# A decoder layer in five overlapped stages: row maxima turned by VectorE and DRAM, setup moved, and matmuls that nobody reads

## The chip, the cores and the metric

The kernel runs on one core of a Trainium2 chip. The metric is the device time of one execution in microseconds (us), lower is better. Engines are called as in the profile: PE (TensorE's matmuls), PEld (its weight loads), DVE (VectorE), ACT (ScalarE), POOL (GpSimd), SP (SyncE, which issues all DMAs here).

## What is computed

x is (32, 256, 256), ctx_1024 is (32, 120, 256). Cut to what matters:

```python
def attn(x):                       # 16 heads of 16, scores of rank 32, causal
    q, k, v = (split_heads(x @ W.T + b) for W, b in ((Wq, bq), (Wk, bk), (Wv, bv)))
    q_lr = einsum('bhtd,hdr->bhtr', q, Wq_lsr); k_lr = einsum('bhtd,hdr->bhtr', k, Wk_lsr)
    a = softmax(where(causal, -inf, einsum('bhir,bhjr->bhij', q_lr, k_lr) / sqrt(32)))
    return merge_heads(einsum('bhij,bhjd->bhid', a, v)) @ Wo.T + bo
def xattn(x, ctx):                 # as given: softmax over the support, then a mask on its rows
    ...
    return out @ proj_w.T + proj_b
def ffn(x):                        # x_prev is x shifted by one token
    r = sigmoid((mu_r * x + (1 - mu_r) * x_prev) @ W_r)
    k = (mu_k * x + (1 - mu_k) * x_prev) @ W_k
    return r * (square(relu(k)) @ W_v)
x = layernorm(x + attn(x)); x = layernorm(x + xattn(x, ctx)); x = layernorm(x + ffn(x))
```

## The kernel before

The 32 batches (256 tokens each) pass through five stages that are skewed against each other. In step t the kernel does IN (projections q and k) for batch t, SCORES for batch t-2, PROBS for t-3, CROSS (output projection, layer norm, cross attention) for t-4 and FFN for t-5. So steps 0 to 4 fill the pipeline, 5 to 31 are full, 32 to 36 (and a rest on the other engines) drain it. Every engine has its own program, the order of which is written out by hand, and the engines meet at semaphores; `Batch.dma_count` and `chunks_done` give the counts. `run_steps` calls `step(t)` and, after step 0, `between`, in which the remaining weights are prepared.

Scores. q and k of a batch (`rows_out_split`, line 474) are split into a high and a low part (ACT `split_hi`, line 675; DVE `split_lo`, line 873), stored to DRAM (`save_parts`, 328) and loaded back as rows per head (`load_stack`, 336, 12 DMAs of 128 KB) into `stack`. PE computes scores in six chunks (`slot`, 522, called in the order 0, 2, 3, 1, 4, 5). In a slot the stage SCORES fills `ps_s` for one batch, from which DVE takes row maxima (`row_maxima`, line 869), and PROBS fills `ps_t` for the batch before it, with the scores turned, from which ACT takes exp (line 673). Each of the two has one buffer of two banks, so a chunk waits for the reader of the one before. The negated maximum of each query, the shift, is part of the PROBS matmul: two rows (its high and its low part) at `ONES_ROW` of `stack[0]` for each half of the heads.

The way of the shift. `row_max` is [128, tile, half, head pair]. After slot 5, PE turns it with two transposes into a bank of `ps_m` (line 623), DVE negates it and splits it (lines 974 to 982) in `shift_parts`, 16 partitions by 2 by 256, and SP issues four DMAs of 8 KB from there into the two rows of each half (line 374). PE's ps_t chunk 0 of the next step waits for them (line 532). Behind them in SP's order stand the 12 loads of `stack` for the batch in stage IN.

Between the slots PE does the projections and the work of CROSS and FFN into two banks `ps_m`, whose users follow each other in a fixed ring (`BANK_USERS`, `bank_free`, line 250). After slot 5 come r3, g, the transposes mT, `PV(0)`, v3, z2, `PV(1)`, kx and vx. `xT` low parts are made by POOL (`x_lo`, line 1065) from ACT's high parts (`x_hi`).

Setup. PE folds the rank matrices and Wq (lines 402 to 417), behind a wait for the bias columns; POOL makes the identity, the block diagonal, constants, the rows of ones of slot 0 of the ring, and the masks, and then x_lo(0). After step 0, `other_weights`: PE folds Wxk with Wxq (427) and makes two constant rows (437 to 441), DVE splits Wv, Wo, Wr, Wkf, Wvf (806, 809) and copies banks (818). SP's step starts with the store of q and loads x of the next batch after the store of k (359).

Of the kernel before, what the change touches and what calls it, by code (L numbers as in the profile page):

```python
# [5 lines left out]
F32 = mybir.dt.float32  # L6
F32R = mybir.dt.float32r
# [18 lines left out]
VW = 32  # L26

# [18 lines left out]
def decoder_layer(nc, x, x_turned, ctx_turned, mask_in, Wq, bq, WkT, bk, WvT, bv, WoT, bo, Wq_lsr_turned, Wk_lsr_turned,  # L46
# [8 lines left out]
    with es:  # L55
# [42 lines left out]
        row_max = sb("row_max", [P, NT, 2, HEADS // 2])  # L98
        shift_parts = sb("shift_parts", [HEADS, 2, T], F32R)
        shift = shift_parts[:, 1, :].bitcast(F32)  # L100
# [13 lines left out]
        BLOCK = 32  # L114
# [46 lines left out]

        ps_s = ps("ps_s", [P, 1024])
# [11 lines left out]
        filled = sems(*["f_" + n for n in ("q", "k", "v", "mT", "z1", "x1T", "s2", "g", "z2",  # L174
# [16 lines left out]
        v_ = sems("q_lo", "k_lo", "shift_done", "shift_hi", "shift_lo",  # L191
# [13 lines left out]
        stack_loaded = [sem(f"stack_loaded{r}") for r in range(RING)]  # L205
        shift_loaded = [sem(f"shift_loaded{r}") for r in range(RING)]
# [23 lines left out]
        def wait(eng, s, count):  # L230

            if count > 0:
# [7 lines left out]
             ("mT", SCORES, v_["shift_done"]), ("z2", CROSS, v_["sum2_done"]), ("vx", PROBS, a_["vx_ready"])],  # L240
# [49 lines left out]
        def run_steps(step, ahead=0, between=None):  # L290

            for t in range(B + LAST_SKEW + ahead):
                step(t)
                if t == 0 and between:
                    between()
# [3 lines left out]
        def _(sp):  # L299
# [46 lines left out]
            def step(at):  # L346
                b = Batch(at, IN)
                if live(at, IN):
                    save_parts(b, 0, "q_lo")
# [7 lines left out]
                if live(at + 1, IN):  # L357
                    sp.wait_ge(g_["xT_lo"], b.n + 1)
                    sp.dma_start(x_in[:], tokens(x_turned, b.n + 1).rearrange("(k p) t -> p k t", p=P)).then_inc(x_loaded, 16)
# [4 lines left out]
                if live(at, SCORES):  # L364
# [25 lines left out]
        def _(pe):  # L390
# [16 lines left out]
            pe.wait_ge(bias_loaded, 16 * 2)  # L407
# [7 lines left out]
            bank = setup_bank()  # L415
            for a in range(KC):
# [5 lines left out]
            def other_weights():  # L422
# [11 lines left out]
                pe.wait_ge(w_ready, len(SPLIT))  # L434
# [7 lines left out]
                assert bank_no[0] == SETUP_TOTAL  # L442
                pe.wait_ge(setup_taken, SETUP_TOTAL)

# [72 lines left out]

            def step(at):
                A, Sb, Pb, X, F = (Batch(at, s) for s in (IN, SCORES, PROBS, CROSS, FFN))
                on = {s: live(at, s) for s in (IN, SCORES, PROBS, CROSS, FFN)}  # L520

                def slot(c):

                    if on[SCORES]:
# [5 lines left out]
                    if on[PROBS]:  # L530
                        if c == T_ORDER[0]:
                            pe.wait_ge(shift_loaded[Pb.slot], Pb.dma_count(4))
# [3 lines left out]
                    if on[SCORES]:  # L536
                        causal_mask(c, ps_s, mask_s, P).then_inc(s_filled, 1)
                    if on[PROBS]:
# [27 lines left out]
                slot(0)  # L566
                if on[IN]:
                    bank = bank_free(pe, "q", at)
                    pe.wait_ge(g_["xT_lo"], A.n + 1)
                    rows_out_split(bank, "Wq", xT[A.slot]).then_inc(filled["f_q"], 1)  # L570
                slot(2)
                if on[CROSS]:
# [3 lines left out]
                slot(3)  # L576
                if on[FFN]:
# [3 lines left out]
                if on[IN]:  # L581
                    bank = bank_free(pe, "k", at)
                    rows_out_split(bank, "Wk", xT[A.slot]).then_inc(filled["f_k"], 1)
# [575 lines left out]
```

## Time and profile before

| | us |
|---|---|
| median of 3 runs | 996.53 (995.14 to 1000.03) |
| the profiled execution | 1001.48 |
| its span, first to last instruction | 999.80 |
| step 0 starts (q of batch 0) | 15.99 |
| steps 5 to 31 | 123.5 to 864.7 |
| steps 32 to the end | 864.7 to 999.8 |
| PE busy in the span | 914.2 (91%) |
| DVE, ACT, POOL busy | 747.6, 592.3, 452.1 |
| mean granted clock of TensorE | 0.951 |

A line of a timeline gives start, duration, engine, line of the kernel, operation, what it writes and reads, its count, and in brackets how long the engine was idle before it and who ended that. In the chain, a line is start, duration and what the last-ending chain of work was doing. PEclk is the granted clock in tenths of full speed (2.4 GHz), so 1.00 and 0.50 are its two levels.

### The profile page before, as it was taken

To read this page: it belongs to the slowest core of one execution; us is meant where nothing else is said; L and a number is where in the kernel's file an instruction comes from. 1 tells how busy PE (TensorE), PEld (TensorE's weight loads), DVE (VectorE), ACT (ScalarE), POOL (GpSimd) and SP (SyncE) were. 2 spreads that over 40 slices of the span, in tenths; PEclk is the share of its full clock that TensorE was granted. 3 is DMA by queue.
4 is the path that set the end of the run, shared out by engine and by line. 5 is a ranking of instruction groups with operands and counts; after the bars stand their busy time and mean duration, and the time that the engine had idled before them with its cause. 6 is when DMAs were issued, how large, how long until landed. Compare 5 with 4: busy or idle time off the path is not lost.

```text
span 999.8 us, 25726 instructions
## 1 busy us (share of the span) xinstructions
PE 914.2 (91%) x9572; PEld 728.0 (73%) x9572; DVE 747.6 (75%) x1565; ACT 592.3 (59%) x1153; POOL 452.1 (45%) x667
## 2 busy tenths in 40 slices
PE   4468999999999999999999999999999999999853
PEld 4346687787777777877877777777777777677652
DVE  3335788888888888888888888888888888767431
ACT  1113567766666666677666666666776666555632
POOL 8100244555445444445554454445454544443443
PEclk9767999999999999999999999999999999989876
DMA  5957667777666666677777666666777776610000
GB/s 162 165 112 132 127 123 144 144 145 144 109 124 115 132 134 130 127 143 144 145 144 127 111 113 135 127 133 129 139 144 145 144 122 110 113 29 28 23 11 21
DMA packets 114791, 118.68 MB, mean 119 GB/s; under 512 B 20649, under 2 KB 98283, under 8 KB 114667
## 3 DMA queue, kind: packets, MB, share of 16 engines
q1 hardware_dynamic: 114667, 117.03, 61.0%
q8 instruction: 77, 1.26, 0.6%
q14 instruction: 47, 0.39, 0.2%
HBM read 74.00 MB, written 41.94 MB: 116 GB/s over the span
## 4 chain that ended last, share of the span: by engine, by line
PE 79%; ACT 8%; issue 5%; DVE 4%; POOL 3%; DMA 1%; SPq 0%; ACTq 0%; POOLq 0%; DVEq 0%
PE ps_m L486 20%; PE ps_m L478 11%; PE ps_o L560 9%; PE ps_s L499 8%; PE ps_t L499 5%; PE ps_s L514 4%; PE ps_m L449 4%; PE ps_m L600 4%; PE ps_m L458 3%; ACT sum L690 3%; ACT p L673 3%; PE ps_m L636 3%; PE ps_m L616 3%; PE ps_m L466 3%; PE ps_t L514 2%
## 5 line engine op out<-in xcount | busy, mean ns | idle before, releaser
L869 DVE TENSOR_REDUCE row_max<-ps_s 128x4 f32<-128x1024 f32 (+1 forms) x192 | 233.1, 1214 | 56.3 <-PE ps_s L514 53.1
L673 ACT ACTIVATE p<-ps_t 128x1024 f32<-128x1024 f32 x192 | 196.1, 1021 | 22.7 <-PE ps_t L514 22.6
L499 PE MATMUL ps_s<-stack 48*128 48x128 f32 (+1 forms) x1024 | 109.0, 312 | 14.4 <-DVE row_max L869 10.6
L1065 POOL TENSOR_TENSOR xT_lo<-x_in,xT_hi 128x512 fp32r<-128x512 f32 x32 | 43.9, 1371 | 165.0 <-ACT xT_hi L660 164.9
L782 ACT COPY kxT<-ps_m 128x240 f32<-128x240 f32 x32 | 11.5, 358 | 178.7 <-PE ps_m L458 178.7
L499 PEld LDWEIGHTS ps_s<-stack 48*128 48x128 f32 x1024 | 73.1, 189 | 50.8 <-DVE row_max L869 22.8
L499 PE MATMUL ps_t<-stack 50*128 50x128 f32 (+1 forms) x1024 | 92.3, 279 | 7.1 <-DMA stack<-shift_parts 4.3
L560 PE MATMUL ps_o<-p,v_pad 128*32 128x256 f32 (+1 forms) x2048 | 98.6, 335 | 0.0
L1104 POOL TENSOR_TENSOR sum<-r_tanh,x 128x512 f32<-128x512 f32 x32 | 40.7, 1271 | 119.6 <-DVE r_tanh L989 119.6
L560 PEld LDWEIGHTS ps_o<-p,v_pad 128*32 128x32 f32 x2048 | 58.6, 111 | 40.8 <-issue 19.5
L499 PEld LDWEIGHTS ps_t<-stack 50*128 50x128 f32 x1024 | 74.8, 191 | 8.9 <-DMA stack<-shift_parts 4.5
L886 DVE BATCH_NORM_STATS2 bn<-sum 128x6 f32<-128x256 f32 x192 | 71.9, 416 | 3.6 <-POOL sum L1104 1.4
L1090 POOL TENSOR_TENSOR xk_lo<-r_tanh,xk_hi 128x512 fp32r<-128x512 f32 x32 | 41.3, 1289 | 66.2 <-ACT xk_hi L727 66.2
L1053 POOL TENSOR_TENSOR rstd<-var,neg_half 128x2 f32<-128x2 f32 x96 | 67.0, 698 | 0.0
L514 PE MATMUL ps_s<-mask_s,identb 64*64 64x256 bf16 (+1 forms) x768 | 66.2, 335 | 0.0
L514 PE MATMUL ps_t<-mask_t,identb 64*64 64x256 bf16 (+1 forms) x768 | 61.7, 311 | 0.0
L1074 POOL TENSOR_TENSOR yT_lo<-y32T,yT_hi 128x512 fp32r<-128x512 f32 x32 | 41.2, 1289 | 44.1 <-ACT yT_hi L698 44.1
L1093 POOL TENSOR_TENSOR xr_lo<-dx,xr_hi 128x512 fp32r<-128x512 f32 x32 | 41.3, 1289 | 40.9 <-ACT xr_hi L743 40.9
L1050 POOL TENSOR_TENSOR var<-mv,eps 128x2 f32<-128x2 f32 x96 | 18.9, 197 | 88.2 <-DVE mv L892 88.0
L478 PE MATMUL ps_m<-xT_hi,hi_Wq 128*128 128x256 f32 x128 | 41.5, 325 | 15.1 <-POOL xT_lo L1065 14.6
L919 DVE SCALAR_TENSOR_TENSOR dx<-dx,cols,x2T 128x256 f32<-128x256 f32 x64 | 53.9, 881 | 0.0
L877 DVE SCALAR_TENSOR_TENSOR parts<-ps_m,cols,parts 128x256 fp32r<-128x256 f32 x64 | 28.0, 479 | 29.3 <-ACT parts L682 29.3
(163 smaller groups left out, 2767.5 us busy)
## 6 DMA issues: line engine op xcount, KB each, us to landing
stack<-parts_dram SPq DMA_DIRECT2D x384, 128.0 KB, 6.0
parts_dram<-parts SPq DMA_DIRECT2D x64, 512.0 KB, 5.7
x_in<-in_x_turned SPq DMA_DIRECT2D x32, 256.0 KB, 5.3
x_res<-in_x SPq DMA_DIRECT2D x32, 256.0 KB, 5.4
out_x<-sum SPq DMA_DIRECT2D x64, 128.0 KB, 6.5
ctxT<-in_ctx_turned SPq DMA_DIRECT2D x32, 120.0 KB, 4.9
stack<-shift_parts SPq DMA_DIRECT2D x128, 8.0 KB
p<-in_Wq SPq DMA_DIRECT2D x1, 256.0 KB, 3.0
```

Source lines behind the costliest of these rows:

```text
L478: last = nc.tensor.matmul(bank[:, a * T:(a + 1) * T], ww, ss, start=(e == 0), stop=(e == len(terms) - 1))
L486: last = nc.tensor.matmul(bank[:, j * C:(j + 1) * C], ss, ww, start=(e == 0), stop=(e == len(terms) - 1))
L499: nc.tensor.matmul(target[:, at_h:at_h + width], left[b.slot][r0:r0 + rows_n, h // 2, rows_at:rows_at + P], right[b.slot][r0:r0 + rows_n, ...
L514: last = nc.tensor.matmul(o, identb[r, 64 * half:64 * half + 64], mask[r, block, 0:o.shape[1], :], start=False, stop=True, skip_group_chec ...
L560: last = nc.tensor.matmul(ps_o[VW * j:VW * (j + 1), half, at_g + T - width:at_g + T], v_pad[b.slot][:, tile, h, :], p[c][:, at_h:at_h + wi ...
L673: nc.scalar.activation(p[c][:], ps_t[:], ACT.Exp).then_inc(exp_done[c], 1)
L869: nc.vector.tensor_reduce(row_max[:, tile, :, j0:j0 + nj], ps_s[:].rearrange("p (g j w) -> p g j w", j=nj, g=2), AX_X, ALU.max) \
L886: last = nc.vector.bn_stats(bn[i][:, j, :], src[:, j, :])
L919: last = nc.vector.scalar_tensor_tensor(dst[:, k, :], dx[:, k, :], cols[:, mu, k:k + 1], x2T[:, k, 0:T], op0=ALU.mult, op1=ALU.add)
L1053: g.tensor_tensor(rstd[i][:], var[i][:], neg_half[:], ALU.pow).then_inc(rstd_done[i], 1)
L1065: g.tensor_tensor(xT[b.slot][1][:], x_in[:], xT[b.slot][0][:].bitcast(F32), ALU.subtract) \
L1090: g.tensor_tensor(xk[1][:], xk_f32, xk[0][:].bitcast(F32), ALU.subtract).then_inc(g_["xk_lo"], 1)
```

## The change

1. **Turned maxima.** `row_max` is laid out as [128, half, head pair, tile]. DVE negates and splits it in place of PE's transposes, still on 128 partitions (two operations on 128x32), and turns both parts in one 32x32-block transpose (128x64). SP stores the two parts to DRAM (two DMAs, 128 pieces of 128 bytes each), waits for them, and loads the rows back (two DMAs, two rows of 8 KB each). The bank user mT goes.
2. **Setup in order of need.** PE waits for the biases only before the product that uses them. POOL does x_lo(0) right after the block diagonal, then the ones of ring slot 0 and constants, x_lo(1), and then the masks; the ones of slots 1 and 2 come after steps 0 and 1. SP loads the next x at the start of its step. The remaining weights come after step 1 (on PE and DVE), the split of the three FFN weights after step 2, and PE waits for these after its step 2. In step 3 the q projection stands between the SCORES part and the PROBS part of slot 0.
3. **Matmuls that nobody reads.** `filler(n)` issues n matmuls of 128x128 by 512 columns in bf16, in step 2 into `ps_t`, in step 3 into `ps_o`, in steps 34 to 36 into `ps_s`, which nobody uses in those steps at that time. By the conditions these are 12, 12, 12, 28 and 25.

```diff
+        shift_parts = sb("shift_parts", [P, 2, NT * HEADS], F32R)
+        shift_turned = sb("shift_turned", [P, 2, BLOCK])
@@ sync, step
+                if live(at + 1, IN):
+                    sp.wait_ge(g_["xT_lo"], b.n + 1)
+                    sp.dma_start(x_in[:], tokens(x_turned, b.n + 1).rearrange("(k p) t -> p k t", p=P)).then_inc(x_loaded, 16)
                 if live(at, IN):
                     save_parts(b, 0, "q_lo")
...
-                    sp.wait_ge(v_["shift_lo"], c.n + 1)
+                    sp.wait_ge(v_["shift_turned"], c.n + 1)
+                    for w in range(2):
+                        sp.dma_start(shift_dram[c.slot][w].rearrange("r b t -> b r t"), shift_turned[:, w, :]) \
+                            .then_inc(shift_saved[c.slot], 16)
+                    sp.wait_ge(shift_saved[c.slot], c.dma_count(2))
                     for g in range(2):
-                        for part in range(2):
-                            r0 = 64 * g + ONES_ROW + part
-                            sp.dma_start(stack[0][c.slot][r0:r0 + 1].bitcast(F32),
-                                         shift_parts[8 * g:8 * g + 8, part, :].bitcast(F32)).then_inc(shift_loaded[c.slot], 16)
+                        r0 = 64 * g + ONES_ROW
+                        rows_g = slice(HEADS * g, HEADS * g + HEADS)
+                        sp.dma_start(stack[0][c.slot][r0:r0 + 2].bitcast(F32),
+                                     shift_dram[c.slot][:, rows_g].rearrange("w r b t -> w (r b t)")) \
+                            .then_inc(shift_loaded[c.slot], 16)
@@ tensor
+            def keep_clock(bank, n):
+                for _ in range(n):
+                    nc.tensor.matmul(bank, identb[:], mask_s[:, 0].rearrange("p n w -> p (n w)"), start=True, stop=True)
...
+                def filler(n, when=True):
+                    if when:
+                        if first_scores:
+                            keep_clock(ps_t[:, 0:512], n)
+                        elif first_probs:
+                            keep_clock(ps_o[:, 0, :], n)
+                        elif scores_over:
+                            keep_clock(ps_s[:, 0:512], n)
...
+                if Pb.n == 0:
+                    slot(0, probs=False)
+                    project("q", "Wq")
+                    slot(0, scores=False)
+                else:
+                    slot(0)
+                    project("q", "Wq")
+                filler(4, scores_over and on[PROBS])
                 slot(2)
+                filler(4, not on[CROSS])
...
                 slot(3)
+                filler(4, not on[FFN] and not on[IN])
...
+                project("k", "Wk")
+                filler(4, scores_over and on[PROBS])
+                filler(12, cross_last)
+                filler(14, ffn_last)
                 slot(1)
...
+                filler(4, scores_over and on[PROBS])
                 slot(4)
+                filler(4, not on[FFN] and not on[CROSS])
...
                 slot(5)
+                filler(4, not on[FFN] and not on[CROSS])
...
-                if on[SCORES]:
-                    bank = bank_free(pe, "mT", at)
-                    pe.wait_ge(max_done[5], Sb.n + 1)
-                    for i in range(NT):
-                        last = nc.tensor.transpose(bank[0:HEADS, i * P:(i + 1) * P],
-                                                   row_max[:, i].rearrange("p g j -> p (g j)"), ident[:])
-                    last.then_inc(filled["f_mT"], 1)
+                filler(7, ffn_last)
                 PV(0)
...
+                filler(16, cross_last)
                 PV(1)
...
-            run_steps(step, between=other_weights)
+            run_steps(step, between={1: other_weights, 2: weights_taken})
@@ vector
                 row_maxima(5)
...
+                    dve.wait_ge(max_done[5], Sb.n + 1)
+                    nc.vector.tensor_scalar(shift_parts[:, 0, :], maxima, -1.0, None, ALU.mult) \
+                        .then_inc(v_["shift_hi"], 1)
+                    dve.wait_ge(v_["shift_hi"], Sb.n + 1)
+                    nc.vector.scalar_tensor_tensor(shift_parts[:, 1, :], maxima, -1.0, shift_parts[:, 0, :].bitcast(F32),
+                                                   op0=ALU.mult, op1=ALU.subtract).then_inc(v_["shift_lo"], 1)
+                    dve.wait_ge(v_["shift_lo"], Sb.n + 1)
                     if prev.n >= 0:
+                        dve.wait_ge(shift_saved[prev.slot], prev.dma_count(2))
+                    nc.vector.transpose(shift_turned[:].rearrange("p w t -> p (w t)"),
+                                        shift_parts[:].rearrange("p w r -> p (w r)").bitcast(F32)) \
+                        .then_inc(v_["shift_turned"], 1)
...
+            run_steps(step, ahead=1, between={1: other_weights, 2: ffn_weights})
@@ gpsimd
+            x_lo(0)
+            pool.wait_ge(g_["xT_lo"], 1)
+            ones_rows(0)
...
+            x_lo(1)
+            pool.wait_ge(g_["xT_lo"], 2)
...
+            run_steps(step, ahead=1, between={0: lambda: ones_next(1), 1: other_weights})
```

## Rows read from the trace of the kernel before

**Rows 1.** The page: busy tenths and granted clock of PE in 40 slices of 25 us.

```profile
PE   4468999999999999999999999999999999999853
PEclk9767999999999999999999999999999999989876
```

**Rows 2.** Waits of PE from 124 to 865 us: who for whom, total, times, longest.

```profile
PE ps_m L449 <- ACT sum L690: 5.2, 27, 0.2
```

**Rows 3.** The chain that ended last, 500 to 528 us: start, us, what.

```profile
500.31 0.22 PE ps_m L623 x2
...
508.43 0.45 PE ps_t L499 x8
```

**Rows 4.** Timeline of DVE, 500 to 529 us.

```profile
500.57 0.41 DVE L974 TENSOR_SCALAR shift_parts<-ps_m 16x256 f32<-16x256 f32 x1 [1.22 <-PE ps_m L623]
...
501.82 1.39 DVE L982 TENSOR_TENSOR shift_parts<-shift_parts 16x256 fp32r<-16x256 f32 x1
...
524.68 0.17 DVE L961 RECIPROCAL s_rec<-s_sum 128x2 f32<-128x2 f32 x1 [1.10 <-ACT a_exp L751]
524.88 0.78 DVE L965 TENSOR_SCALAR a_nrm<-a_exp,s_rec 128x120 f32<-128x120 f32 x2
525.59 1.21 DVE L869 TENSOR_REDUCE row_max<-ps_s 128x4 f32<-128x1024 f32 x1
```

**Rows 5.** Timeline of SP's issues, 500 to 600 us.

```profile
530.69 2.70 SPq L374 DMA_DIRECT2D stack<-shift_parts  x4
```

**Rows 6.** The chain from 0 to 135 us: the first shift.

```profile
70.15 1.91 DMA stack<-shift_parts
```

**Rows 7.** DMA queue 520 to 530 us (packets, MB, share); then stretch 32 to 34 (clock, share, GB/s).

```profile
q1 hardware_dynamic: 1355, 1.41, 40.4%
...
32.00:34.00 2.00, 0.50 1.16 136
```

**Rows 8.** Waits of PE from 0 to 125 us.

```profile
PE ps_m L478 <- POOL xT_lo L1065: 14.6, 2, 8.1
```

**Rows 9.** Timeline of all engines, 0 to 24 us.

```profile
5.42 1.81 DVE L806 TENSOR_SCALAR hi_Wk<-p 128x512 fp32r<-128x512 f32 x1 [0.71 <-DMA p<-in_WkT]
...
6.29 0.62 ACT L660 CAST xT_hi<-x_in 128x512 fp32r<-128x512 f32 x1 [4.22 <-DMA x_in<-in_x_turned]
...
6.79 2.05 PE L412 MATMUL ps_s<-yu,p 128*128 128x128 f32 x8 [2.61 <-DMA cols<-in_bk]
...
14.58 1.26 POOL L1065 TENSOR_TENSOR xT_lo<-x_in,xT_hi 128x512 fp32r<-128x512 f32 x1
...
15.99 0.55 PE L478 MATMUL ps_m<-xT_hi,hi_Wq 128*128 128x256 f32 x1 [6.50 <-POOL xT_lo L1065]
```

**Rows 10.** The chain from 0 to 135 us: setup after step 0, steps 1 and 2.

```profile
29.15 3.75 PE ps_o L437 x8
...
35.41 4.53 PE ps_m L478 x24
...
48.94 2.90 PE ps_m L478 x12
```

**Rows 11.** The chain from 850 to 1000 us: 12 matmuls at either clock.

```profile
883.40 1.41 PE ps_m L478 x12
...
937.06 2.57 PE ps_m L478 x12
```

**Rows 12.** Waits of PE from 921 to 1000 us.

```profile
PE ps_m L478 <- POOL xk_lo L1090: 5.0, 1, 5.0
PE ps_m L449 <- ACT x L690: 4.5, 1, 4.5
PE ps_m L449 <- ACT sum L690: 4.2, 2, 3.7
...
PE ps_t L499 <- ACT p L673: 2.8, 2, 1.7
PE ps_m L486 <- POOL yT_lo L1074: 2.4, 1, 2.4
```

More of the change, by code:

```diff
@@ L171, in sems @@
             return {n: sem(n) for n in names}
[L174 removed]
+        filled = sems(*["f_" + n for n in ("q", "k", "v", "z1", "x1T", "s2", "g", "z2",
                                            "kx", "vx", "x2T", "k3", "r3", "v3")])
@@ L205, in decoder_layer @@
         stack_loaded = [sem(f"stack_loaded{r}") for r in range(RING)]
+        shift_saved = [sem(f"shift_saved{r}") for r in range(RING)]
         shift_loaded = [sem(f"shift_loaded{r}") for r in range(RING)]
@@ L293, in run_steps @@
                 step(t)
-                if t == 0 and between:
-                    between()
+                if between and t in between:
+                    between[t]()
         @block.sync
@@ L564, in PV, with project @@
                     last.then_inc(o_filled[half], 1)
[L566 to L570, printed above, removed]
+                def project(what, w):
+                    if on[IN]:
+                        bank = bank_free(pe, what, at)
+                        pe.wait_ge(g_["xT_lo"], A.n + 1)
+                        rows_out_split(bank, w, xT[A.slot]).then_inc(filled["f_" + what], 1)
+                if Pb.n == 0:
[6 more added lines that the diff above has]
+                filler(4, scores_over and on[PROBS])
                 slot(2)
+                filler(4, not on[CROSS])
                 if on[CROSS]:
@@ L999, in step @@
                 attention_out(1)
-            run_steps(step, ahead=1, between=other_weights)
+            run_steps(step, ahead=1, between={1: other_weights, 2: ffn_weights})
         @block.gpsimd
@@ L1031, in ones_rows @@
                     pool.wait_ge(ones_ready[r], h + 1)
-            ones_rows(0)
-            link(g.tensor_copy(identb[:], ident[:]))
-            link(g.memset(mask_s[:], 0.0))
-            link(g.memset(mask_t[:], 0.0))
-            for half in range(2):
-                r = slice(64 * half, 64 * half + 64)
-                for m, sign in ((mask_s, 1), (mask_t, -1)):
-                    link(g.affine_select(out=m[r], in_=m[r], compare_op=ALU.is_ge, fill=MASKED, base=0,
-                                         pattern=[[64 * sign, 2], [0, 4], [-sign, P]], channel_multiplier=sign))
-            g.memset(x2T[:, :, 0:1], 0.0).then_inc(consts_ready, 1)
-            pool.wait_ge(consts_ready, 1)
             def inverse_deviation(i, b):
@@ L1106, in step, with ones_next @@
                     inverse_deviation(1, X)
+            def ones_next(r):
+                pool.wait_ge(g_["xT_lo"], r + 1)
+                ones_rows(r)
             def other_weights():
+                ones_next(2)
                 pool.wait_ge(setup_taken, SETUP_TOTAL)
-            x_lo(0)
-            pool.wait_ge(g_["xT_lo"], 1)
-            for r in range(1, RING):
-                ones_rows(r)
-            run_steps(step, ahead=1, between=other_weights)
+            run_steps(step, ahead=1, between={0: lambda: ones_next(1), 1: other_weights})
 SETUP_FIRST = 3
```

92 lines of the change are left out of this document (55 added, 37 removed).

## Prediction

> **What bounds the kernel now.** I read the slices of the page first, then the waits of TensorE, then the chain, and only then single steps. The slices [rows 1] show three parts: a start in which PE is busy 4 to 8 tenths and its clock wanders, a long middle at 9 tenths and full clock, and an end in which both fall. In the middle (124 to 865 us, 27 steps of 741.3/27 = 27.45 us) the waits of PE hold one entry, 5.2 us in 27 times [rows 2]. So a middle step is bound by PE's own instructions: what leaves its queue shortens the step, what is saved on DVE does not. The rest of the gain can only lie in the 123 us before and the 135 us behind.
>
> **The turned maxima, middle.** Two transposes of row_max stand in PE's queue in each step: 0.22 us of the chain [rows 3]. They go. 27 x 0.22 = 6.0 us, and about 0.4 + 0.2 + 0.2 in steps 4, 32 and 33: together **6.9 us**. The bank that they used had its next user (z2) wait for DVE; that wait is now for r_tanh, which is older, so nothing.
>
> On DVE three operations on 16 partitions go, of which two took 0.41 and 1.39 us (the third is a cast between them), and 1.22 us of idling before them [rows 4]. In come two operations on 128x32 and a transpose of 128x64. No row shows them; the smallest like them, 128x2, takes 0.17 us, one on 120 columns about 0.39, so three lie between 0.5 and 1.2; I take 0.75 with the gaps, near the small one since 32 columns are few. DVE gets lighter by some 2.5 us a step, worth nothing in the middle, since no wait of PE on DVE is left there.
>
> The price is on the way back to stack. Before, the shift took four DMA issues of 0.63 to 0.70 us on SP from 530.69 on [rows 5], and in the first step the last of them, issued at 70.15, landed after 1.91 us [rows 6]. Now it takes two stores to DRAM, a wait on SP, and two loads. Queued behind that wait on SP are the 12 loads of stack (0.5 us of issuing each), needed only two steps later. Who waits for the shift is PE, at ps_t's first chunk of the next step (508.43 is one of them [rows 3]).
>
> Budget: the last row maximum of a step ends at 525.59 + 1.21 = 526.80 [rows 4]. The next ps_t chunk is due at 508.43 + 27.45 - 0.22 = 535.66. That leaves **8.9 us**. The new way: DVE 0.75; two issues 2 x 0.65, the second starting at 1.4; landing of the second 1.9 after that if small pieces cost nothing (3.3); SP starts the loads, the second at 4.0, landing at 5.9. The pieces are new: each store is 128 pieces of 128 bytes. In 520 to 530 us, 1355 packets took 40.4% of 16 engines for 10 us, 0.048 us of an engine each; the stack loads in 32 to 34 us ran at 136 GB/s in pieces of 1 KB at a share of 1.16, which is 0.14 us of an engine each [rows 7]. Spread over 16 engines the 256 pieces cost 16 x 0.048 to 0.14 = 0.8 to 2.2 us: the way takes 6.7 to 8.1 us and fits. If a transfer is dealt out by its leading dimension (4 in the stores), they cost on four engines 64 x 0.048 = 3.1 us (way about 8.0 to 9.0) to 64 x 0.14 = 9.0 us (way 14). I take 0.05 us a piece, as the pieces are smaller than both, and so the way fits, with a slack of 0.5 to 2 us. The fall-back is the rival below.
>
> The Trainium skill, "DMA: Bandwidth & Descriptors", section on why a DMA increments its semaphore by 16, says that the number of engines is the largest up to 16 that divides the slowest dimension of both access patterns. The stores write with a leading dimension of 4 against 128 partitions, so by it 4 engines; the loads lead with 2, so 2 engines. No run here shows it.
>
> **Setup in order of need.** PE's first waits [rows 8] are 14.6 us for xT_lo in two places; 2.6 for a bias column come before the fold [rows 9]. (a) The fold of Wq no longer waits for the bias: it starts near 4.9 instead of 6.79. xT_hi(0) is there at 6.91, but POOL made masks first and began xT_lo only at 14.58, so q began at 15.99 [rows 9]. Now POOL takes xT_lo at about 6.95, ready 8.2; DVE splits Wk 5.42 to 6.6 (its 1.81 us beside POOL's memset [rows 9] shrinks to the 0.42 of later splits), Wq from 6.95 to 8.4. q(0) starts at 8.6: **7.4 us** earlier. (b) Then POOL has 3.65 + 0.65 + 0.4 + 1.9 us of ones and memsets, until 15.1; x_in(1), now first in SP's step, is issued at 11.8 and lands at about 15.7 (x_in(0), whose xT_hi began at 6.29 [rows 9], was issued at 2.7 and took 3.6), xT_lo(1) ends at 17.7, and q(1), k(1) take 17.8 to 23.0. (c) The other weights come after step 1: splits of Wv and Wo end at about 28 (they now share the time with a memset of POOL's), L437 to L441 took 5.8 of the 6.3 us between 29.15 and 35.41 [rows 10], so step 2 starts at 34 or, at full clock, 31.5. stack(0): the stores of parts, about 3 us each after 13.0 and 15.6, are followed by loads of 12 x 128 KB, 11.5 us at 136 GB/s [rows 7], so it is there at 28: not last. x_in(2) was held up behind SP's wait for k_lo(1), and q(2) began at 48.94 [rows 10]. Now it is issued at 22.3 behind the stack loads, lands at about 29, xT_lo(2) ends at 31. q(2) follows slot 0 at about 35: **14 us** earlier than 48.94, between 12 and 16.
>
> (d) Step 2 from q(2) to its last maximum took 17.1 us, to 66.05. Same work, plus 12 fillers. The granted clock of the slices from 25 to 100 us was 0.6 to 0.7 [rows 1], so over half of the time it stood at the low one of its two levels, 1.2 GHz. What that costs: 12 matmuls of 256 columns take 2.57 us low and 1.41 full [rows 11], so a filler of 512 columns is 0.24 us full and 0.43 low. Four fillers fill 0.95 us of a wait of 1.24 for row_max at full clock, and overrun it by 0.5 at the low one. The low-clock work in step 2 (half of k, slot 1, v, slot 4) is some 6.7 us, 3 over full; I credit half, 1.5. Last maximum at 50.7. (e) Behind it DVE has 0.75 of shift and three more splits, 3.15, on which PE's weights_taken waits: PE starts step 3 at +3.9 instead of +0.6, does slot 0's scores and q(3) (1.1 + 2.6 at low clock) to +7.6, and the shift lands at about +7 to +8. Before, ps_t began at +6.1 and slot 2 at +10.6; now slot 2 starts at about +9.2: 1.4 us. (f) The rest of step 3, 22.2 us, loses the 0.7 us in which PV(0) stood behind the maxima, and has 5 us of low-clock cost, of which I credit 2.8. Sum of the start: 14 + 1.5 + 1.4 + 3.5 = 20.4, say **20 us** (14 to 22).
>
> **The last steps.** PE idles 2.4 us before z1 of step 35, 3.7 before its x1T, 4.6 before x2T and 5.0 before k3 of step 36, and twice for exp in step 34 [rows 12], with low-clock work after most. Step 34 gets 4 + 4 + 4 fillers: the first eight lie in the waits for exp, 1.1 and 1.7 us; the last four come on top (1 us) but the work after, x1T, a slot, s2 and k3, would run at full clock (2.9 us less): 2 us. Step 35 has 12 fillers in the 3.7 us before x1T, which keep s2, k3 and r3 at full clock: k3 alone 1.16, s2 0.96, r3 0.4, and 2.5 in all reach v3. The next 16 and 4 lie in the wait before x2T, 4.8 us at full clock in 4.6: about even. Step 36: k3 1.16, r3 0.75, v3 0.4, of which 2 reach the end. Together 6.5, and with half of a miss, **6 us** (0 to 9).
>
> **Sum.** 6.9 + 20 + 6 = 32.9 us. The profiled execution took 1001.48 (span 999.80 and 1.68 around it), so 968.6 on its own terms. The median of the runs is 996.53, 4.95 lower, which puts the sum at 963.6. The start has most links counted, each of which can only be late for a reason not seen; I take 2.4 us off it: **966 us**.
>
> **Rivals.**
> 1. The shift arrives late (slower). Place: ps_t's first chunk of every step from 3 to 34. Point: the way is over 8.9 us, which on four engines is a price of about 0.06 to 0.075 us a piece. Price: at 0.10 us, 64 x 0.05 = 3.2 us more than taken, an overrun of about 2.3 us; 31 steps x 2.3 = 71 us against 32.9: about 1035. For it: the stack loads' 0.14 us, and DRAM as target of 128-byte pieces. Against: the queue is empty at that time and the other row says 0.048. It ends slower from an overrun of 1.1 us on. By the page named above, with 0.048 it just fits and with 0.14 it gives 5 us and more a step.
> 2. A small overrun, 0.2 to 0.8 us a step (mean 0.45): 31 x 0.45 = 14 us back, 980. The slots behind would hide part of it, since PE's order is fixed and only the chunk waits.
> 3. The start moves its wait: x_in(2) or the stack loads land late in the fuller queue, or the fillers overrun at the low clock (half of 89 fillers x 0.2 = 9 us). Gain of the start 11, of the end -2: 6.9 + 11 - 2 = 16, 980.
> 4. The fillers do not hold the clock. Then they cost where no wait covers them, 2 us, and the start keeps 15: 996.5 - 6.9 - 15 + 2 = 977. For it: before, the slices of the start have PE busy 8 tenths from 75 to 100 us and still a clock of 0.7 [rows 1]. Against: the full middle never fell.
>
> The Trainium skill, "TensorE: Matmul & The Clock Gate", section on the HAM clock gate, says activity releases the throttle and idling brings it back; the lower clock of the last slices [rows 1], where PE idles, agrees. The credit above is worked out from rows at the two levels alone.
>
> **How the numbers follow.** Forecast as summed: 0.62. Rival 1: 0.12. Rival 2: 0.11. Rival 3: 0.08. Rival 4: 0.07. The likeliest one's own range is 954 to 976. For 8 in 10 it reaches to rivals 2 to 4: **953 to 986**; above lies rival 1. A measurement of this kernel can tell about 0.5% (5 us) from no change. Faster by more than that: forecast, rivals 3 and 4, rival 2 nearly all: 0.86. Within: 0.04. Slower: 0.10, the upper part of rival 1.
>
> **What would show it.** Middle step 27.45 down to 27.23 us; the waits of PE in it still with x1T alone and no entry of ps_t on the stack DMA (with one, rival 1 or 2, its size by times is the overrun). q(0) at 8.6, q(2) at 35, step 4 starting near 79 to 80 instead of 98.85. In the last 70 us the granted clock full in most stretches, where it stood at 0.5 to 0.8. From the last maximum to the last load landing 6.5 to 8.5 us. Wrong would make it: pieces dearer than 0.065 us on few engines, or setup work on DVE and POOL that collides more than the one memset allowed for.

## The result and the profile after

| | before | after | ratio (95% interval) |
|---|---|---|---|
| first measurement, median us | 995.84 (4 runs) | 969.54 (4 runs) | 0.9725 [0.9677, 0.9773] |
| second measurement, median us | 996.53 (11 runs) | 973.56 (6 runs) | 0.9755 [0.9711, 0.9800] |

The forecast was 966.0, range 953 to 986. The ten executions after lie in two groups with nothing between: four from 961.56 to 965.76 us and six from 973.25 to 975.97. The profiled one of the first measurement took 973.32 us (span 971.6), that of the second 961.56 (span 959.8). The first median, 969.54, is the mean of 965.76 and 973.32, so no execution took it. The mean granted clock of each execution is on record too: 0.982 to 0.987 in the four, 0.967 to 0.975 in the six. Both profiles are shown, since the difference between them is the point that the prediction missed.

The stretches, from the copies of vx that end each step's work on PE (us):

| stretch | before | after, first | after, second |
|---|---|---|---|
| start to end of step 3 | 99.0 | 82.3 | 76.2 |
| step 4 | 24.5 | 24.9 | 25.2 |
| steps 5 to 31 (27) | 741.3 | 735.7 | 735.7 |
| steps 32 to 34 | 85.4 | 83.2 | 78.6 |
| the rest | 49.6 | 45.6 | 44.1 |
| span | 999.8 | 971.6 | 959.8 |

The slices of the page answer to [rows 1]: first those of the first measurement's profile, then PE and the clock of the second's.

```profile
PE   6789999999999999999999999999999999999975
...
PEclk9959999999999999999999999999999999989998
```

```profile
PE   6778999999999999999999999999999999998975
...
PEclk8989999999999999999999999999999999999998
```

PE is now busy 9 tenths from the fourth slice on (from the fifth in the second profile). In the first profile the third slice has a clock of 0.5 at a PE that is busier than in the second, where it is 0.8.

**Middle.** The waits of PE from 107 to 842 us of the change (waited for, us in total, times, longest) answer to [rows 2]:

```profile
PE ps_m L463 <- ACT sum L735: 5.2, 27, 0.2
```

It is the one entry, as before: no step of the middle waits for the shift. Its chain in one middle step (start, us, what) has no row_max transpose where [rows 3] had one:

```profile
514.94 0.87 PE ps_m L480 x4
515.81 0.59 PE ps_s L513 x8
516.40 0.45 PE ps_t L513 x8
```

The whole way of the shift stands in the chain at the end of step 3, where PE did wait for it:

```profile
77.81 0.19 DVE shift_parts L1021
...
78.03 0.20 DVE shift_parts L1024
...
78.25 0.26 DVE shift_turned L1029
...
78.53 0.55 SPq L378
...
79.12 1.91 DMA shift_dram<-shift_turned
...
81.05 0.28 SPq L384
...
81.38 1.96 DMA stack<-shift_dram
...
83.38 0.66 PE ps_t L513 x8
```

From DVE's first operation to the chunk it is 5.57 us. In the middle step above the last maximum ended at 507.55, the last update of the loads' semaphore came at 513.47 in the trace, and the chunk starts at 516.40. So the way is 5.9 us there (5.7 to 6.3 in the 27 middle steps), and the slack 2.9 us (2.4 to 3.0, median 2.8), where 0.5 to 2 was forecast.

**Start.** The timeline of the first profile (start, us, what, idle before and who ended it) answers to [rows 9] and [rows 10]:

```profile
7.14 1.27 POOL L1100 TENSOR_TENSOR xT_lo<-x_in,xT_hi 128x512 fp32r<-128x512 f32 x1 [4.53 <-ACT xT_hi L705]
...
9.16 0.58 PE L492 MATMUL ps_m<-xT_hi,hi_Wq 128*128 128x256 f32 x1 [0.91 <-DVE bq_fold L863]
...
17.59 0.36 PE L492 MATMUL ps_m<-xT_hi,hi_Wq 128*128 128x256 f32 x1 [2.94 <-POOL xT_lo L1100]
...
24.47 2.10 DVE L851 TENSOR_SCALAR hi_Wv<-p 128x512 fp32r<-128x512 f32 x1
...
34.15 0.36 PE L492 MATMUL ps_m<-xT_hi,hi_Wq 128*128 128x256 f32 x1
...
46.47 1.22 DVE L918 TENSOR_REDUCE row_max<-ps_s 128x4 f32<-128x1024 f32 x1 [0.84 <-PE ps_s L528]
...
52.62 1.12 PE L513 MATMUL ps_s<-stack 48*128 48x128 f32 x8 [5.23 <-DVE lo_Wvf L854]
```

q(0), q(1) and q(2) start at 9.16, 17.59 and 34.15, and step 2's last maximum ends at 47.69. Then PE idles 5.23 us for the splits of the FFN weights. What follows is in the stretches: us, busy time of PE, PEld, DVE, ACT, POOL with counts, then PEclk, DMA share and GB/s. First profile, then the second:

```profile
34.00:46.00 12.00, 10.36 (x88) 7.22 (x84) 7.69 (x9) 2.33 (x6) 3.60 (x2) 1.00 1.12 144
...
48.00:52.50 4.50, 0.00 (x0) 0.00 (x0) 4.36 (x8) 0.15 (x1) 1.46 (x1) 0.62 0.42 140
52.50:72.00 19.50, 18.99 (x115) 13.63 (x116) 6.57 (x9) 5.66 (x8) 0.00 (x0) 0.50 0.88 149
```

```profile
48.00:52.20 4.20, 0.00 (x0) 0.01 (x1) 3.92 (x10) 0.00 (x0) 0.42 (x1) 0.74 0.10 22
52.20:57.00 4.80, 4.77 (x28) 4.02 (x30) 1.23 (x1) 0.00 (x0) 0.00 (x0) 0.52 0.88 139
57.00:72.00 15.00, 13.54 (x152) 8.59 (x153) 7.94 (x11) 8.78 (x13) 0.00 (x0) 1.00 0.91 179
```

In both the clock falls to its lower level while PE waits. In one it stays there for 19.5 us with PE 97% busy, in the other it is back after some 5 us. Of the 6.1 us between the two ends of step 3, 0.4 were there when PE resumed (52.62 and 52.23); the other 5.7 come in this stretch.

**End.** The waits of PE from 845 us to the end answer to [rows 12]:

```profile
PE ps_s L513 <- DVE row_max L918: 5.0, 4, 1.4
PE ps_m L500 <- POOL yT_lo L1140: 2.4, 1, 2.4
PE ps_m L492 <- POOL xk_lo L1156: 2.1, 1, 2.1
...
PE ps_m L463 <- ACT sum L735: 0.8, 1, 0.8
```

xk_lo shrank from 5.0 to 2.1 and sum from 4.2 to 0.8 (2.4 in the second profile): the unread matmuls stand there. yT_lo is as before, and nothing was put there.

### The profile page after: what moved, and what is told of

The parts are those of the page before. It is cut to its first block, busy times and chain, and to the rows that moved or that the text cites. A ratio compares the mean times of both kernels' runs of the same rounds, so it can differ in the third digit from the quotient of the medians.

```text
span 971.6 us, 25805 instructions
## 1 busy us (share of the span) xinstructions
PE 918.1 (94%) x9597; PEld 723.6 (74%) x9597; DVE 715.0 (74%) x1565; ACT 590.1 (61%) x1153; POOL 450.6 (46%) x667
## 4 chain that ended last, share of the span: by engine, by line
PE 80%; ACT 8%; issue 5%; DVE 4%; POOL 2%; DMA 1%; SPq 0%; ACTq 0%; POOLq 0%; DVEq 0%
PE ps_m L500 20%; PE ps_m L492 11%; PE ps_o L594 9%; PE ps_s L513 8%; PE ps_t L513 5%; PE ps_s L528 4%; PE ps_m L463 4%; PE ps_m L649 3%; PE ps_m L472 3%; ACT p L718 3%; ACT sum L735 3%; PE ps_m L680 3%; PE ps_m L666 3%; PE ps_m L480 3%; PE ps_t L528 2%
## 5 line engine op out<-in xcount | busy, mean ns | idle before, releaser
L1100 POOL TENSOR_TENSOR xT_lo<-x_in,xT_hi 128x512 fp32r<-128x512 f32 x32 | 41.4, 1293 | 151.4 <-ACT xT_hi L705 151.4
L594 PE MATMUL ps_o<-p,v_pad 128*32 128x256 f32 (+1 forms) x2048 | 96.3, 329 | 0.0
L952 DVE STREAM_TRANSPOSE yu<-ps_o 128x512 f32<-128x512 f32 x64 | 44.8, 701 | 16.6 <-PE ps_o L594 16.6
```

The source lines that it names most:

```text
L594: last = nc.tensor.matmul(ps_o[VW * j:VW * (j + 1), half, at_g + T - width:at_g + T], v_pad[b.slot][:, tile, h, :], p[c][:, at_h:at_h + wi ...
L952: nc.vector.transpose(turned, ps_o[:, half, :]).then_inc(yu_turned[half], 1)
L1100: g.tensor_tensor(xT[b.slot][1][:], x_in[:], xT[b.slot][0][:].bitcast(F32), ALU.subtract) \
```

## The experiments

Eleven measurements, in three groups of runs; two of them repeat a kernel. Where the text compares medians of different groups, it goes by the ratio to the kernel before in the same group.

### Turned maxima alone

The kernel before with `row_max` as [128, half, pair, tile], DVE's three new operations, two stores and two loads in SP, and PE's two transposes gone; setup as before, no unread matmul.

> The kernel before with the turned maxima alone (stores and loads through DRAM, no transposes on TensorE). Theory: the gain is the 0.21 us a step of TensorE's queue that the middle of the changed kernel shows, and about 1 us in steps 3 and 4: 6 to 7 us, ratio about 0.9935, middle step 27.25 us, no wait of TensorE for the shift in the middle. Rival: the lighter VectorE or the longer way through DRAM shows too: then more than 9 us, or less than 4 us with a wait of ps_t on the load of the shift.

Measured: 988.59 us, ratio 0.9894 [0.9859, 0.9929], 10.5 us less. Its 27 middle steps took 735.7 us as in the full change (27.247 each, before 27.455): 5.6 us. The 6 to 7 us expected were exceeded, as by the rival. The profiles differ by 15.4 us, and the rest stands in steps that the edit explains little of: step 3 ended at 91.2 in place of 99.0 and step 32 took 26.4 in place of 31.1, but step 4 took 27.5 in place of 24.5. Between 60 and 100 us the shift came late twice, 5.2 us before step 3 (4.3 in the kernel before) and 1.7 before step 4:

```profile
PE ps_t L509 <- DMA stack<-shift_dram: 6.9, 2, 5.2
```

That is 2.6 us more than before, about as much as the edit saved there: PE's wait for the last maxima before its transposes, 2.7 us in steps 2 and 3 of the kernel before, is gone. What made the start shorter is the clock: the 24 projection matmuls of step 1 took 4.53 us before [rows 10] and 3.09 here, the 64 of PV in step 3 5.08 and 2.81. Why the clock was higher is open.

Over the profiles of all kernels without added stores, step 32 takes from 26.4 to 31.1 us (31.1 in the kernel before and in setup alone, 26.4 to 26.6 in five others). The waits of PE in it are the same in this kernel, in the one before and in the change (the first line below), and yet the clock behind the second of them fell in the kernel before (second line) and not here (third):

```profile
PE ps_s L509 <- DVE row_max L872: 2.5, 2, 1.4
```

```profile
874.00:882.00 8.00, 7.41 (x52) 6.13 (x56) 3.44 (x6) 4.90 (x9) 2.96 (x4) 0.57 0.42 93
```

```profile
864.00:872.00 8.00, 8.00 (x85) 6.72 (x78) 6.84 (x11) 6.88 (x16) 4.03 (x3) 1.00 0.12 36
```

The two profiles of the change differ in the same way (29.4 and 26.4 us): behind the same two waits of at most 1.4 us the clock falls in one execution and not in the next. So nothing ties the 4.7 us of step 32 to this edit, and of its gain only the middle's 5.6 is explained by it.

### Setup alone, and the change without unread matmuls

"Setup alone" is the changed kernel with PE's transposes and the old four DMAs put back and with the loop of `keep_clock` at zero. "No fill" is only the latter:

```diff
-                for _ in range(n):
+                for _ in range(0):
                     nc.tensor.matmul(bank, identb[:], ...)
```

> The changed kernel with the old transposes on TensorE and with no matmuls that nobody reads: setup in order of need alone. Theory: q of batch 0 begins at 9.2, q of batch 2 near 34 to 35, and the gain is 14 to 16 us (ratio 0.985), all of it before step 5. Rival: without the extra matmuls the clock falls in steps 2 and 3 and gives back 5 us or more: gain 9 to 11 us.

> The changed kernel without the matmuls that nobody reads. Theory: they are worth about 6 us in the last three steps and 2 to 3 us in steps 2 and 3, so this takes 8 to 9 us more than the changed kernel: about 978, ratio 0.982. Rival: they hold the clock at the end only, or nothing at all; then 0 to 6 us more, 970 to 975.

Measured: setup alone 988.23, ratio 0.9895 [0.9845, 0.9944], 10.8 us less; no fill 976.9, ratio 0.9788 [0.9743, 0.9833], 22.1 less. The two parts add up: 10.5 + 10.8 = 21.3. Setup alone gained less than the 14 to 16 us expected and what its rival said (9 to 11). Its stretches, in the slowest of its six executions, say why: q(2) starts at 35.2, but PE is at the lower clock through step 2 and much of step 3. No fill met the expected time; by ratio it takes 3 to 6 us more than the change, where 8 to 9 were expected.

```profile
30.00:40.00 10.00, 9.25 (x40) 6.28 (x39) 2.77 (x4) 1.46 (x3) 4.86 (x3) 0.50 1.05 212
40.00:60.00 20.00, 11.93 (x74) 9.11 (x74) 11.19 (x18) 2.00 (x5) 1.27 (x1) 0.59 0.58 112
60.00:76.00 16.00, 14.08 (x101) 10.76 (x100) 6.39 (x8) 5.28 (x8) 0.00 (x0) 0.61 1.06 162
```

### Unread matmuls in the last steps alone

```diff
-                        if first_scores:
-                            keep_clock(ps_t[:, 0:512], n)
-                        elif first_probs:
-                            keep_clock(ps_o[:, 0, :], n)
-                        elif scores_over:
+                        if scores_over:
                             keep_clock(ps_s[:, 0:512], n)
```

> The changed kernel with the extra matmuls in the last three steps only (none in steps 2 and 3). Theory: 2 to 3 us more than the changed kernel, 972, since in the traced run of it the clock was low from 50 to 73 us anyway although TensorE was busy. Rival: the 24 of steps 2 and 3 are what lets the clock rise before step 3 in the quicker runs (964 and 966 against 973 and 976): then this stays at 975 or more in all runs.

Measured: 973.33, ratio 0.9757 [0.9704, 0.9809], 3.6 us under no fill, with intervals that overlap. The profiles say more: step 34 and the rest took 68.5 us, against 75.9 in no fill and 75.8 before, so the 65 matmuls are worth up to 7.4 us there; in the two profiles of the full change that stretch took 71.5 and 68.4. Against the full change (0.9725 and 0.9755) the medians tell no difference. The profiles do tell one for the twelve in step 2: from the start of q(2) to the last maximum of the step it was 17.0 us here, 16.9 in no fill and 18.5 in setup alone, all without them, and 13.5 and 13.6 in the change (13.6 to 15.3 in the six other kernels and repeats that have them). From 30 to 49 us, first here and then in the change's first profile:

```profile
30.00:49.00 19.00, 16.16 (x94) 12.51 (x92) 7.32 (x10) 3.14 (x8) 4.86 (x3) 0.68 1.09 208
```

```profile
30.00:49.00 19.00, 15.75 (x114) 10.10 (x112) 10.93 (x17) 3.56 (x8) 5.50 (x4) 0.95 1.09 217
```

So they keep the clock up and shorten step 2 by about 2 to 3 us. The medians don't show it; the clock's other differences from one execution to the next are larger.

### PE's transposes put back into the change

> The changed kernel with the old transposes on TensorE and the old four loads; setup and extra matmuls kept. Theory: a middle step is back at 27.45 us and the time is 6 to 8 us more than the changed kernel, about 976. Rival: in step 3 the old way of the shift hides better behind q of batch 3, so that only 4 us are lost.

Measured: 976.78, ratio 0.9788 [0.9763, 0.9813]. The middle is back at 27.468 us a step (741.6 in all), 5.9 more than the change; the whole is 3 to 6 us more by ratio, where 6 to 8 were expected. With the first experiment this shows the term of the middle from both sides.

### How much slack the way of the shift has

The two stores are done twice, or three times, each round behind a wait for the one before, which makes the way longer by a known amount.

```diff
-                    sp.wait_ge(shift_saved[c.slot], c.dma_count(2))
+                    sp.wait_ge(shift_saved[c.slot], c.dma_count(4) - 32)
+                    for again in range(1):
+                        for w in range(2):
+                            sp.dma_start(shift_dram[c.slot][w].rearrange("r b t -> b r t"), shift_turned[:, w, :]) \
+                                .then_inc(shift_saved[c.slot], 16)
+                        sp.wait_ge(shift_saved[c.slot], c.dma_count(4) - 32 + 32 * (again + 1))
```

> The changed kernel with both stores of the shift issued and awaited a second time before the loads: one more round, about 2.5 us, on the way of the shift. Theory: in the middle the loads land about 3.3 us before ps_t needs them, so a middle step stays at 27.25 us and only step 3, where TensorE waited 0.5 us already, gets 2 to 3 us longer: 971 to 973. Rival: the way is as tight as forecast (slack 0.5 to 2 us): then 0.5 to 2 us a step more, 985 to 1030.

> The same with two more rounds, about 5 us. Theory: slack 3.3 us, overrun 1.7 us in each of the 31 steps: 50 us more, about 1020, with waits of ps_t on the load of the shift of 1.7 us. Rival: the slack is larger, since later slots give the time back: then under 20 us more.

Measured: one round more 982.59, ratio 0.9850 [0.9818, 0.9882]; two rounds more 1109.55, ratio 1.1116 [1.1079, 1.1153]. Both missed what was expected (971 to 973, and about 1020). A round is 2.5 us (stores issued at 512.68 and again at 515.19, loads at 517.65). Waits of PE in the middle, first with one round more, then with two (110 to 960 us), and the 27 middle steps of the latter as a stretch:

```profile
PE ps_m L468 <- ACT sum L740: 5.3, 27, 0.2
PE ps_t L518 <- DMA stack<-shift_dram: 2.8, 3, 1.8
```

```profile
PE ps_t L518 <- DMA stack<-shift_dram: 60.2, 27, 4.2
```

```profile
115.55:969.04 853.49, 784.22 (x7994) 624.46 (x7995) 592.20 (x1294) 497.11 (x970) 361.15 (x537) 0.93 0.63 117
```

The same 27 steps in the change:

```profile
107.20:842.80 735.60, 726.71 (x7994) 581.96 (x7994) 592.61 (x1294) 492.19 (x969) 361.71 (x537) 1.00 0.72 134
```

With 2.5 us more the middle steps took 27.447 in the mean, 0.2 longer, and the chunk waited in three of 27. 3.5 of these 5.4 us are in step 5; 22 of the other 26 took 27.2 to 27.3 as before, so the 2.5 is just inside the slack: of 2.8 us 0.3 are left, by the same updates. The 3.3 that both expectations took for the slack was worked out from the way of step 3, 5.57 us, and is 0.5 too high. What else the first expectation lacked stands around them: step 4 took 29.2 in place of 24.9, with a wait of 3.4 us for the shift, and step 5 30.8, with one of 1.8. With 5 us more a step took 31.61, 4.4 longer. 5.0 less the slack of 2.8 is 2.2, which is what a simple overrun would cost, and the recorded waits are 60.2/27 = 2.2 us. The rest is the clock: its mean in this stretch is 0.93, where it is 1.00 in the middle of the kernel before and of the change. For the same matmuls PE is busy 784.2 us in place of 726.7, which is 2.1 us a step. The two make the 4.4 measured. So an overrun is paid twice: once as the wait, and once as low clock after it. The chain shows it right behind one of these waits: twelve matmuls at 498.70 took 2.86 us, where the same twelve take 1.63 at full clock.

```profile
495.13 2.11 DMA stack<-shift_dram
...
497.28 0.66 PE ps_t L518 x8
...
498.70 2.86 PE ps_m L497 x12
```

### Unread matmuls over the wait before step 3

```diff
             def weights_taken():
+                keep_clock(ps_t[:, 0:512], 22)
                 pe.wait_ge(setup_taken, SETUP_TOTAL)
                 pe.wait_ge(w_ready, len(SPLIT))
```

> The changed kernel with 22 more extra matmuls where TensorE waits 5.2 us for the last split weight after step 2. In the traced run of the changed kernel the granted clock fell there (at about 49 us) and stayed at 0.50 until 73 us, with TensorE busy from 52.6 on. Theory: the fall comes from this wait; with it filled, step 3 runs at full clock and 8 to 10 us go in those runs that were slow: 962 to 966 in all runs. Rival: the low stretch has another cause than the idle time and stays: no change of the median, and the spread of 964 to 976 stays.

> The changed kernel with 22 more matmuls that nobody reads in PE's wait before step 3, a second time, in the same call as the changed kernel itself. If the low clock of step 3 comes from that wait in most executions: 3 to 7 us below the changed kernel. If the low clock was an accident of the one profiled execution (the clock of step 3 differs from run to run without a cause): within 2 us of it.

> The changed kernel a second time, as the measure for the other two of this call. By the first measurement 969.5, within 964 to 976; step 3's clock low after the 5.2 us wait again if the wait causes it (step 3 ends near 82), high (step 3 ends near 76 to 79) if it was chance.

Measured: 967.68, ratio 0.9694 [0.9664, 0.9723], and the second time, beside the change itself, 968.47, ratio 0.9727 [0.9697, 0.9757], against the change's 973.56 and 0.9755 [0.9711, 0.9800]. The first was expected at 962 to 966 in all executions, and only two of its six are; the second was expected 3 to 7 us below the change and came out 5.1 below. The clock holds from 48 to 76 us in both its profiles; those of the first:

```profile
48.00:53.00 5.00, 5.00 (x25) 2.25 (x24) 4.83 (x9) 0.55 (x1) 1.27 (x1) 1.00 0.43 147
53.00:72.00 19.00, 17.16 (x187) 11.26 (x188) 10.21 (x15) 8.88 (x13) 0.18 (x1) 1.00 0.87 176
```

The splits end at 53.75 and 52.26, no earlier than in the change (52.51 and 52.12), and yet step 3 ends at 75.8 and 74.8 in place of 82.3 and 76.2. The gap stands empty in eight profiles: two of the change, and one each of setup alone, no fill, the last steps alone, the transposes put back, and the two with longer stores. In all eight the clock is low behind it, in six for 4 to 6 us after PE resumed and in two for about 20; in the three profiles with unread matmuls in it (the third is of the next experiment) it isn't. So the low clock of step 3 comes from PE's idling before it; how long it lasts afterwards differs from one execution to the next. The second long one is that of the unread matmuls in the last steps alone, with PE 92% busy:

```profile
57.60:76.00 18.40, 16.89 (x107) 12.94 (x107) 6.56 (x8) 5.66 (x8) 0.00 (x0) 0.50 0.93 168
```

By what was expected of the change's second profile, an end of step 3 at 76 to 79 us meant chance, and it came at 76.2. But the clock had fallen there all the same, and came back sooner; that both could be so, the expectation left out.

The Trainium skill, "TensorE: Matmul & The Clock Gate", section on the HAM clock gate, says that idling brings the throttle back and that activity releases it. The first half agrees with all of these traces. The second doesn't agree with the first profile, where PE was 97% busy for 19.5 us at the low level; the measurement decides, and the matmuls really were that slow, since step 3 ended 6.1 us later.

The twelve executions with the gap filled lie between 964.77 and 971.95: none as slow as the change's six from 973.25 on, and none as fast as its two at 961.56 and 962.75. The profiled 961.56 had full clock in steps 32 and 34 and the rest as well (26.4, 24.4 and 44.1 us), where the two profiles with the gap filled took 27.9 and 29.4, 27.4 and 25.9, 46.2 and 45.6. Nothing in the edit touches those steps. By ratio to the kernel before, the filled gap is 0.3% better than the change in each of the two measurements, with intervals that overlap: that it lowers the median is likely and not shown; that it keeps the clock up in step 3 is.

### The wait for the FFN weights moved behind q(3)

```diff
             def weights_taken():
                 pe.wait_ge(setup_taken, SETUP_TOTAL)
-                pe.wait_ge(w_ready, len(SPLIT))
@@ step
                     slot(0, probs=False)
                     project("q", "Wq")
+                    keep_clock(ps_t[:, 0:512], 22)
+                    pe.wait_ge(w_ready, len(SPLIT))
                     slot(0, scores=False)
```

> The changed kernel with the wait for the FFN weights moved behind step 3's first scores and q(3), and 22 matmuls that nobody reads between q(3) and that wait. Theory (what bound the entry into step 3 is the way of the shift, not the splits): the shift of the kernel with 22 matmuls in the gap was ready at 50.59 us, its loads were issued at 53.23 and 0.56 later, so they land at about 55.8, against 56.40 for its first transposed scores. So 0.6 to 1 us less than that kernel, about 967, with the granted clock at 1.00 through step 3. Rival (PE's order is the bound and the shift has slack): the transposed scores start at 52.5 to 53.5 and the time is about 964.

Measured: 970.81, ratio 0.9746 [0.9714, 0.9777], no better than the filled gap. Both expectations missed the start of the transposed scores:

```profile
53.84 0.56 SPq L384 DMA_DIRECT2D stack<-shift_dram  x2
```

```profile
53.09 4.92 PE L534 MATMUL ps_t<-mask_s,identb 128*128 128x512 bf16 x22
57.94 0.66 PE L512 MATMUL ps_t<-stack 50*128 50x128 f32 x8
```

By the updates of their semaphore in the trace the loads had landed at 56.70. The rival's 52.5 to 53.5 is out. But the 22 unread matmuls, sized for a wait of 5 us, ran to 57.9 and held up PE for 1.2 us themselves. That is how a filler loses: by (56.7 - 53.09) / 0.22, 16 would have been enough, which no run tried. The rest of the theory follows by arithmetic only: with the gap filled, the loads had landed at 55.76 and the chunk started at 56.40, so the shift is the next bound, 0.6 us behind the splits' wait.

## Why the prediction was right, and where its terms were off

The time was right within 4 us by the first measurement and 8 by the second. The middle was right by its mechanism. That the start and the end came out near their sums too is in part luck: step 2 was better than forecast by 3 us, and what the gap before step 3 does to the clock was not in the sum. By its own steps, against the two profiles of the change:

- **Middle**, 6.0 forecast, 5.6 measured in both, and confirmed by two experiments. That PE's own queue is the bound there [rows 2], so that 0.22 us off it is 0.2 us off the step, held. 0.209 came out for 0.22.
- **The way of the shift**, about 8 us forecast, 5.57 measured in step 3 and 5.9 in the middle. Mis-sized was the price of a piece, 0.05 us of an engine. The two stores of a middle step, 508.5 to 511 us (packets, then the queue with its MB and share of 16 engines), and under them two stores of out_x, 128 pieces of 1 KB each, in 950 to 956 us:

```profile
DMA packets 265, 0.05 MB, mean 20 GB/s; under 512 B 264, under 2 KB 264, under 8 KB 264
...
q1 hardware_dynamic: 264, 0.03, 8.5%
```

```profile
DMA packets 288, 0.26 MB, mean 44 GB/s; under 512 B 32, under 2 KB 288, under 8 KB 288
```

  The 264 packets took 0.085 x 16 x 2.5 / 264 = 0.013 us of an engine each, a quarter of the 0.05 taken from [rows 7], whose packets were mostly larger. The number of engines can be read too: out_x has 256 pieces and 32 small packets beside them, 16 a DMA; the shift's stores have 256 pieces and 8 more, 4 a DMA. If the small ones are the counts to the semaphore, one from each engine, out_x runs on 16 engines and a store of the shift on 4. The loads' semaphore got four updates from DMAs, two for each load. That agrees with the rule of "DMA: Bandwidth & Descriptors" of the Trainium skill (section on why a DMA increments its semaphore by 16), which also says that each engine in use posts such a count. 4 and 2 are what the prediction worked out from it. On four engines the pieces cost 64 x 0.013 = 0.8 us in place of 64 x 0.05 = 3.2: the spread was right, the price wrong. DVE's three operations took 0.70 with the gaps (0.75 forecast), the second store landed 1.91 us after SP began to issue it, no later than the last of the old DMAs [rows 6], so its pieces added nothing that shows, and the loads' issue took 0.28 each in place of 0.65 [rows 5]. The way was also to be 6.5 to 8.5 us from the last maximum to the last landing, and this sign of the forecast missed too, as it was 5.6 in step 3 and 5.7 to 6.3 in the middle.
- **Rival 1 and 2** (the shift late) did not come: slack 2.8 us. The price that rival 1 named was too low, though: an overrun of 2.2 us cost 4.4 us a step, since low clock follows the wait.
- **Start**, 20 forecast, 16.7 and 22.8 measured by the end of step 3. The links to q(2) held: 9.16 for 8.6, 17.59 for 17.8, 34.15 for 35. hi_Wv beside POOL's memset took 2.10 us and not 0.42, but that was allowed for (splits of Wv and Wo over at 28.4 for 28). Step 2 after q(2) was better than forecast: its last maximum ended at 47.7 for 50.7, as the clock stood at 1.00 there. The step that failed in part is (e): PE's start of step 3 behind the splits was named (+3.9 from the last maximum; it came to +4.9 and +4.1), but not that the wait takes the clock down for what follows. (f) credited 2.8 us for less low-clock work in step 3; in the first profile there was more of it than in the kernel before (a mean clock of 0.66 from 52.6 to 82.3 us, where that had 0.73 from 72.1 to 99.0), in the second less (0.90 from 52.2 to 76.2). Step 4, forecast 0.4 us shorter, took 0.3 and 0.6 longer.
- **End**, 6 forecast for the fillers; 4.3 and 7.4 measured in step 34 and the rest, 7.4 with the matmuls of the last steps alone. In step 34 four of them ran at the low clock in the first profile, 1.91 us in place of 1.04 for the same four in step 2, and held up the work behind them. The first profile gained 6.2 us in all from step 32 on, of which 1.7 are in step 32, where the change does next to nothing.
- **Rival 3** (the start moves its wait) came in part: the wait went from xT_lo to the weights, though not by a fuller queue or by fillers that overrun. **Rival 4** (fillers don't hold the clock) fell: with the gap before step 3 filled the clock stood at 1.00, with it empty it went down each time. At the end they don't hold it throughout: it was low in step 34 of the first profile, as above.

The sum of 32.9 us lies between the two profiles' 28.2 and 40.0. The forecast named the mechanisms, but took the clock as a credit in each stretch; it is a state that a single gap sets for the next 4 to 20 us. That this is what puts the executions in two groups, 961.6 to 965.8 and 973.3 to 976.0, fits the mean clocks of all ten executions, and the one profile of each group, which differ by 6.1 us up to the end of step 3 and by 6.1 from step 32 on. In which stretch the other eight lost their time isn't known.

## What to carry to other kernels

A wait of PE of 4 to 5 us costs more than itself: look at the granted clock behind it, and put unread matmuls over it up to its end and not beyond (22 where 16 were wanted lost 1.2 us). A detour of a small tensor through DRAM, three operations of DVE with it, was 5.6 to 6.3 us here from the last maximum to the landing, and free if the reader comes later than that; find the slack by doubling the transfer, since beyond it the loss here was twice the overrun, 4.4 us for 2.2. Where the executions of one kernel lie in two groups, read a profile of each before a term is called wrong.

## What the runs showed of the hardware that was not expected

- Behind two waits of PE of at most 1.4 us (2.5 in all) in step 32 the clock came down in some executions and not in others: step 32 took 26.4 to 31.1 us.
- With PE 97% busy, the granted clock stayed at 0.50 for 19.5 us after a wait of 5.2 us; after a wait of 4.4 us of the same program it was back in about 5. Eight profiles with such a wait have six short returns and two long ones.
- The same split of one weight (lo_Wr, 128x512) took 1.64 us on DVE in the first profile and 0.69 in the second; in the first, POOL was at work at that time (1.46 us in 48 to 52.5). It made PE's wait 0.8 us longer.
- A store of 128 pieces of 128 bytes took 0.52 us to issue (median of 64), a load of two rows of 8 KB 0.27, and the second of either landed 1.9 to 2.3 us after SP began to issue it, in step 3 and in the middle step above.
